# Window and linear attention with butterfly FFN on one core: the order of each instruction's waits, and where the layer norm's small steps run

## The chip, the cores and the metric

One NeuronCore of a Trainium2 chip. The metric is the device time of one launch in microseconds. The engines are PE (TensorE), DVE (VectorE), ACT (ScalarE), POOL (GpSimd) and SP, which here issues DMAs.

## The reference, cut to what matters

The input is x, 32 sequences of 256 tokens with 128 features, in float32. Four blocks with residuals run over it, each behind a layer norm without scale or shift:

```python
def _layernorm(x, axis=-1, eps=1e-05):
    m = jnp.mean(x, axis=axis, keepdims=True)
    v = jnp.var(x, axis=axis, keepdims=True)
    return (x - m) / jnp.sqrt(v + eps)

x = x + window_attention(_layernorm(x))   # 16 heads of 8, 2 KV heads, windows of 32, softmax
x = x + butterfly_ffn(_layernorm(x))      # 128 -> 512, butterfly, gelu, butterfly, -> 128
x = x + linear_attention(_layernorm(x))   # phi = elu + 1, k'v per sequence, normaliser + 1e-6
x = x + butterfly_ffn(_layernorm(x))      # the same weights again
```

The butterflies are linear and hang on the weights alone, so the kernel first multiplies them into two weight matrices (the products named `X.`), while the first tokens are already under way.

## The kernel before, in words

The 8192 tokens are cut into 16 groups of 512, each as 4 tiles of 128 tokens. A group passes through stages, and each engine works on several groups at once, shifted against each other: in its turn t an engine does, for every step, the group `t - lag`. `due(t, lag, first, last)` gives that group, and the body of each engine's `turn(t)` is the order of its steps, written out by hand. Letters name the places of a group: P (input, window attention), W (behind window attention, first FFN), F (behind the FFN, linear attention), L (behind linear attention, second FFN), G (result). `x_W` is the residual stream there, `xn_W` its normed form, `xb_W` the stream with the next bias.

Every wait between instructions is written by hand. `Count` turns "event E of group g" into a semaphore value, from tables (`PRODUCTS`, `VECTOR`, ...) that repeat the order in which an engine finishes its events. `eng.wait_ge(semaphore, value)` holds the next instruction. A machine instruction carries one wait. In the built program the one that is written first in the code rides on the instruction, and each further one becomes a wait instruction of its own ahead of it. In the listings below the last name in a `[waits ...]` list is the one that the instruction carries. Where two waits on one semaphore follow each other they are still two.

The layer norm of a group, before: DVE takes `bn_stats` of 4 tiles and `bn_aggr` of 4 tiles (`moments`, L1212 and L1217), which gives mean and variance in `mv`. POOL (`normalise`, L443 to L455) adds epsilon (`rv`), negates the mean (`nm`), raises to -0.5 (`rstd`), multiplies (`nmr`), and writes the 4 tiles of `xn`. For the first group's P and the last group's F and L, DVE writes `xn` instead (L1225). PE then transposes `xn` (L572). There are 64 such norms. DVE adds the residual (`residual`, L1240) when a product is done, ACT copies transposes out (L960) and takes gelu (L982). The softmax of a tile on DVE is: merge the halves (L1255), maximum (L1262), subtract (L1268), transpose (L1275). The heads' outputs are transposed (L1282), the sums inverted (L1286) and divided (L1289). PE writes the scores of a tile at L601 and needs for the next tile that L1268 is done.

Of the kernel before, what the change touches and what calls it, by code (L numbers as in the profile page):

```python
# [9 lines left out]
ALU = mybir.AluOpType  # L10
# [5 lines left out]
HEADS, KV, HD = 16, 2, 8  # L16
# [51 lines left out]
    ("P.bn", 1, 2, 15), ("P.mv", 1, 2, 15), ("W.max3", 3, 1, 1), ("W.cp0", 2, 0, 0), ("W.max0", 2, 0, 0), ("W.cp3", 3, 2, 15),  # L68
    ("W.cp3", 3, 0, 0), ("W.ot2", 4, 0, 1), ("W.rs2", 4, 0, 1), ("W.ot2", 4, 2, 15), ("W.rs2", 4, 2, 15), ("W.tr0", 2, 0, 0),
    ("P.bn", 0, 0, 1), ("P.mv", 0, 0, 1), ("W.max3", 3, 0, 0), ("W.max3", 3, 2, 15), ("F.bn", 5), ("F.mv", 5),  # L70
# [3 lines left out]
    ("W.tr1", 2, 0, 1), ("W.max0", 2, 2, 15), ("W.bn", 4, 0, 1), ("W.mv", 4, 0, 1), ("W.bn", 4, 2, 15), ("W.mv", 4, 2, 15),  # L74
# [18 lines left out]
NORMED = [
    ("W.xn", 5, 2, 15), ("L.xn", 7, 0, 14), ("P.xn", 0, 0, 1), ("P.xn", 1, 2, 15), ("F.xn", 5, 0, 14), ("W.xn", 4, 0, 1),
]
BIASED = [
    ("F.xb", 6), ("P.xb", 3, 2, 15), ("W.xb", 5, 0, 1), ("L.xb", 7), ("W.xb", 5, 2, 15), ("P.xb", 1, 0, 1),
]
PARTED = [
    ("W.um3", 4, 0, 0), ("W.um2", 4, 0, 1), ("W.um2", 4, 2, 15), ("W.um3", 4, 1, 15), ("W.um0", 3, 2, 15), ("W.um1", 3, 0, 1),  # L100
    ("W.um0", 2, 0, 0), ("W.um0", 3, 1, 1), ("W.um1", 3, 2, 15),
]
TURNS = NG + 14
# [8 lines left out]
    ("L.kv", "L.k0"), ("L.kv", "bank"), ("L.oT", "L.out0"), ("L.out0", "L.q"), ("L.out1", "L.kv"),  # L112
    ("L.out1", "L.q"), ("L.proj", "bank"), ("L.q", "L.xT"), ("P.kv", "bank"), ("W.PV0", "bank"),
# [21 lines left out]
class Count:  # L135
# [1474 lines left out]
```

## Time and profile before

| | |
|---|---|
| time, median of 3 runs | 561.26 us (560.38 to 562.34) |
| span of the profiled execution | 560.6 us |
| time of that execution | its span; the median of the three runs is 0.7 us above it |
| PE busy | 525.0 us |
| POOL busy | 450.9 us |
| DVE busy | 441.2 us |
| ACT busy | 358.7 us |
| mean granted TensorE clock | 0.978 of 2.4 GHz |

The span runs from the first instruction to the last. Busy time is what the engine's instructions cover. The busy end of a matmul is modelled, so that a PE without idle time is one that always had its next matmul there.

### The profile page before, as it was taken

The numbers are of one execution on the slowest core, as the hardware profiler recorded it, in microseconds if no ns is written. First come the engines' busy times: TensorE is split into PE (matmuls) and PEld (weight loads), VectorE is DVE, ScalarE is ACT, GpSimd is POOL, SyncE is SP. The second block draws the span as 40 slices with busy tenths as digits, with TensorE's granted clock in tenths as the row PEclk, the third lists the DMA queues.
The fourth block names the chain that finished last, engine by engine and source line by source line (L and its number), as shares of the span: only waits on it lengthen the run. The fifth ranks groups of instructions, "written<-read, shape, count | busy, mean of one in ns | idle before, by whom it ended". The sixth has DMA issues, their size and how long they took to land. (4 is left out here: it accounts for less than half of the span.)

```text
span 560.6 us, 14708 instructions
## 1 busy us (share of the span) xinstructions
PE 525.0 (94%) x5060; PEld 345.8 (62%) x5060; DVE 441.2 (79%) x1272; ACT 358.7 (64%) x578; POOL 450.9 (80%) x646
## 2 busy tenths in 40 slices
PE   5786998979999999999999999999999999999795
PEld 3442554546766666666667676666666667777563
DVE  5778789897888989898988898888989797663341
ACT  2543376567687767676777768686767777664532
POOL 6665689899898999999898989899999797955420
PEclk9789799989999999999999999999999999999899
DMA  9533232322223232232313231323232222100001
GB/s 310 170 76 81 63 83 54 81 74 56 54 58 80 62 76 66 68 78 48 102 45 87 63 87 44 84 60 77 61 76 50 59 66 58 39 1 20 1 20 37
DMA packets 49546, 38.88 MB, mean 69 GB/s; under 512 B 12352, under 2 KB 38976, under 8 KB 49472
## 3 DMA queue, kind: packets, MB, share of 16 engines
q1 hardware_dynamic: 47024, 33.73, 23.9%
q10 hardware_dynamic: 2448, 4.22, 2.1%
q8 instruction: 40, 0.66, 0.5%
q14 instruction: 34, 0.28, 0.2%
HBM read 15.64 MB, written 5.51 MB: 38 GB/s over the span
## 5 line engine op out<-in xcount | busy, mean ns | idle before, releaser
L501 POOL TENSOR_TENSOR probs_t<-probs_t,first 128x1024 f32<-128x1024 f32 x64 | 151.3, 2367 | 11.5 <-DMA probs_t<-probs_t 11.5
L645 PEld LDWEIGHTS ring<-w,early 128*128 128x128 f32 x1024 | 119.0, 192 | 9.6 <-issue 7.0
L982 ACT ACTIVATE early<-ring,b 128x512 f32<-128x512 f32 x128 | 87.2, 684 | 54.7 <-PE ring L633 53.1
L645 PE MATMUL ring<-w,early 128*128 128x128 f32 x1024 | 120.0, 275 | 0.8 <-ACT early L982 0.8
L972 ACT ACT_TABLE_LOAD x58 | 74.4, 1283 | 10.7 <-issue 9.7
L601 PE MATMUL ps_s<-kx,q_t 64*32 64x512 f32 x960 | 65.9, 606 | 3.4 <-DVE merged L1268 2.7
L633 PE MATMUL ring<-xT_G,w1b 128*128 128x512 f32 x128 | 67.1, 612 | 0.7 <-ACT xT_G L960 0.7
L991 ACT ACTIVATE probs_t<-merged_t 128x1024 f32<-128x1024 f32 x64 | 65.3, 1044 | 3.8 <-DVE merged_t L1275 3.7
L633 PE MATMUL ring<-xT_F,w1b 128*128 128x512 f32 x128 | 59.9, 611 | 0.4 <-ACT xT_F L960 0.4
L1255 DVE COPY_PREDICATED ps_s<-first,ps_s 128x512 f32<-128x512 uint32 x64 | 43.6, 681 | 9.2 <-PE ps_s L601 9.0
L1282 DVE STREAM_TRANSPOSE ps_o<-ps_o 128x512 f32<-128x512 f32 x64 | 46.2, 722 | 1.6 <-PE ps_o L618 0.3
L1268 DVE TENSOR_TENSOR merged<-ps_s,rowmax 128x512 f32<-128x512 f32 x64 | 44.1, 689 | 4.1
L618 PE MATMUL ps_o<-probs_t,vx 64*32 64x256 f32 x1024 | 42.3, 387 | 2.5 <-DVE o_w L1289 2.5
L1275 DVE STREAM_TRANSPOSE merged_t<-merged 128x512 f32<-128x512 f32 x64 | 44.2, 696 | 0.4
L1262 DVE TENSOR_REDUCE rowmax<-ps_s 128x16 f32<-128x512 f32 x64 | 43.2, 676 | 1.0 <-issue 0.2
L633 PEld LDWEIGHTS ring<-xT_F,w1b 128*128 128x128 f32 x128 | 23.4, 192 | 25.2 <-issue 20.4
L676 PEld LDWEIGHTS ring<-later,xT_L 128*128 128x128 f32 x128 | 23.0, 189 | 21.6 <-issue 19.0
L676 PE MATMUL ring<-later,xT_L 128*128 128x256 f32 x128 | 34.5, 392 | 0.7 <-ACT xT_L L960 0.7
L618 PEld LDWEIGHTS ps_o<-probs_t,vx 64*32 64x32 f32 x1024 | 15.3, 106 | 27.8 <-issue 22.7
L960 ACT ACTIVATE xT_F<-ring 128x512 f32<-128x512 f32 x16 | 9.6, 597 | 34.5 <-PE ring L572 34.5
L455 POOL TENSOR_SCALAR xn_W<-x_W,rstd_W,nmr_W 128x128 f32<-128x128 f32 x64 | 27.9, 451 | 3.2 <-PE ring L676 2.3
L471 POOL TENSOR_TENSOR xb_F<-x_F,later 128x512 f32<-128x512 f32 x16 | 20.6, 1285 | 12.3 <-DVE x_L L1240 12.1
(124 smaller groups left out, 1023.9 us busy)
## 6 DMA issues: line engine op xcount, KB each, us to landing
probs_t<-probs_t SPq DMA_DIRECT2D x256, 64.0 KB, 2.0
kx<-kv_rows SPq DMA_DIRECT2D x120, 40.0 KB, 2.2
x_P<-in_x SPq DMA_DIRECT2D x16, 256.0 KB, 3.2
out_x<-x_G SPq DMA_DIRECT2D x16, 256.0 KB, 2.4
vx_t<-kv_rows SPq DMA_DIRECT2D x128, 8.0 KB
up_s<-in_up_m ACTq DMA_DIRECT2D x7, 256.0 KB, 8.4
down_s<-in_down_m ACTq DMA_DIRECT2D x7, 256.0 KB, 8.4
kv_rows<-kv_t SPq DMA_DIRECT2D x16, 80.0 KB, 2.8
```

The source lines that it names most:

```text
L501: nc.gpsimd.tensor_tensor(parts, parts, keep.rearrange("p (a t) -> p a t", a=1).to_broadcast([P, PAIR * HEADS, WIN]), ALU.mult).then_inc(p ...
L601: last = nc.tensor.matmul(ps_s[32 * i:32 * i + 32, a], q_t[half, P * j + 32 * c:P * j + 32 * c + 32], keys[half, :, TSPAN * j + 32 * c:TSP ...
L618: last = nc.tensor.matmul(ps_o[32 * c:32 * c + 32, a, 0:HPK * WIN], vx[rows, j, a, s], probs_t[rows, j, s, a], start=True, stop=True)
L633: nc.tensor.matmul(bank(name)[:], w1b[:, P * c:P * (c + 1)], x_t[s][:], start=True, stop=True).then_inc(product.sem, 1)
L645: last = nc.tensor.matmul(bank(name)[:, P * j:P * (j + 1)], hid[s][:, c, P * j:P * (j + 1)], w2[:, c], start=(c == 0), stop=(c == CH - 1))
L676: last = nc.tensor.matmul(bank(name)[:, 2 * P * i:2 * P * (i + 1)], x_t["L"][:, P * j:P * (j + 1)], wl_s[:, P:3 * P], start=True, stop=True)
L972: nc.scalar.activation(unused[:, i:i + 1], half[0:1, 0:1], function)
L982: nc.scalar.activation(hid[s][:, c], bank(name)[:], ACT.Gelu, bias=b1[:, c:c + 1]).then_inc(drained[BANK[name]].sem, 1)
L991: nc.scalar.activation(probs_t[:, j].rearrange("p s k h t -> p s (k h t)"), scores.to_broadcast([P, PAIR, HEADS * WIN]), ACT.Exp).then_inc ...
L1268: nc.vector.tensor_tensor(merged[:, j % 2].rearrange("p k h t -> p (k h) t"), halves()[0], m, ALU.subtract).then_inc(drained["S"].sem, 1)
L1275: nc.vector.transpose(merged_t[:, j % 2].rearrange("p k h t -> p (k h t)"), merged[:, j % 2].rearrange("p k h t -> p (k h t)")).then_inc(v ...
L1282: nc.vector.transpose(ps_o[:, :, 0:HPK * WIN], ps_o[:, :, 0:HPK * WIN]).then_inc(vec.sem, 1)
```

## The change

Four things, and nothing else:

1. At most instructions with several waits, the order of the `wait_ge` calls is turned, so that another semaphore, as a rule that of the step just before it or of the other engine's product, is written first and rides on the instruction. Two waits on the same semaphore are joined to one with the larger value (`Count.both`).
2. Epsilon is added on DVE, right behind `bn_aggr` (`variances_raised`).
3. POOL's norm is one `rstd` and four tiles of `xn` as (x - mean) * rstd. `nm` and `nmr` are gone.
4. The turns are counted from another start (all the lags and tables change with it), and steps are written in smaller functions. In the built programs the order of instructions is the same on PE, ACT and SP, and on DVE and POOL the same but for points 2 and 3.

The core of the diff:

```diff
+    def both(self, *events):
+        return max(self.value(group, name) for group, name in events)
...
+            def rooted_variance(g, s):
+                pool.wait_ge(vec.sem, vec.after(g, f"{s}.rv"))
+                if g == 0:
+                    pool.wait_ge(half_set, 1)
+                nc.gpsimd.tensor_tensor(rstd[s][:], rv[s][:], half[:], ALU.pow).then_inc(rooted.sem, 1)
             def normalise(g, s):
-                pool.wait_ge(vec.sem, vec.after(g, f"{s}.mv"))
-                pool.wait_ge(pool_step.sem, pool_step.after(g - 1, f"{s}.nmr"))
-                nc.gpsimd.tensor_scalar(rv[s][:], mv[s][:, :, 1], LN_EPS, None, ALU.add
-                                        ).then_inc(pool_step.sem, 1)
-                nc.gpsimd.tensor_scalar(nm[s][:], mv[s][:, :, 0], -1.0, None, ALU.mult).then_inc(pool_step.sem, 1)
-                pool.wait_ge(pool_step.sem, pool_step.after(g, f"{s}.rv"))
-                nc.gpsimd.tensor_tensor(rstd[s][:], rv[s][:], half[:], ALU.pow).then_inc(pool_step.sem, 1)
-                pool.wait_ge(pool_step.sem, pool_step.after(g, f"{s}.nm", f"{s}.rstd"))
-                nc.gpsimd.tensor_tensor(nmr[s][:], nm[s][:], rstd[s][:], ALU.mult).then_inc(pool_step.sem, 1)
...
+                rooted_variance(g, s)
+                pool.wait_ge(rooted.sem, rooted.after(g, f"{s}.rstd"))
                 pool.wait_ge(product.sem, product.after(g - 1, TURNED[s]))
-                pool.wait_ge(pool_step.sem, pool_step.after(g, f"{s}.nmr"))
                 for j in range(TILES):
-                    last = nc.gpsimd.tensor_scalar(xn[s][:, j], x_of(g, s)[:, j], rstd[s][:, j:j + 1],
-                                                   nmr[s][:, j:j + 1], ALU.mult, ALU.add)
+                    last = nc.gpsimd.tensor_scalar(xn[s][:, j], x_of(g, s)[:, j], mv[s][:, j, 0:1],
+                                                   rstd[s][:, j:j + 1], ALU.subtract, ALU.mult)
...
             def copy_out(g, name, dst, *freed):
-                act.wait_ge(product.sem, product.after(g - 1, *freed))
-                act.wait_ge(product.sem, product.after(g, name))
+                act.wait_ge(product.sem, product.both((g, name), *((g - 1, user) for user in freed)))
...
             def gelu(g, s, c):
+                act.wait_ge(product.sem, product.both((g, name), (g - 1, f"{s}.down")))
                 if g == 0:
                     act.wait_ge(b1_made, 1)
-                act.wait_ge(product.sem, product.after(g - 1, f"{s}.down"))
-                act.wait_ge(product.sem, product.after(g, name))
...
+            def variances_raised(g, s):
+                dve.wait_ge(vec.sem, vec.after(g, f"{s}.mv"))
+                nc.vector.tensor_scalar(rv[s][:], mv[s][:, :, 1], LN_EPS, None, ALU.add).then_inc(vec.sem, 1)
...
             def residual(g, s, name, base):
+                dve.wait_ge(product.sem, product.after(g, name))
                 if s == "G":
+                    dve.wait_ge(biased.sem, biased.after(g, f"{base}.xb"))
                     dve.wait_ge(y_out.sem, y_out.after(g - 1, "G.y"))
                 else:
+                    dve.wait_ge(biased.sem, biased.both((g, f"{base}.xb"), (g - 1, f"{s}.xb")))
                     dve.wait_ge(normed.sem, normed.after(g - 1, f"{s}.xn"))
-                    dve.wait_ge(biased.sem, biased.after(g - 1, f"{s}.xb"))
-                dve.wait_ge(biased.sem, biased.after(g, f"{base}.xb"))
-                dve.wait_ge(product.sem, product.after(g, name))
...
             def row_max(g, j):
+                dve.wait_ge(vec.sem, vec.after(g, f"W.cp{j}"))
                 dve.wait_ge(drained["S"].sem, drained["S"].after(g - 1, f"W.S{j}"))
-                dve.wait_ge(vec.sem, vec.after(g, f"W.cp{j}"))
```

The wait instructions that stand by themselves go from 355 to 79 on ACT, from 638 to 527 on DVE, from 200 to 140 on POOL, from 65 to 63 on SP and from 248 to 251 on PE.

VectorE in a middle turn, before, from the residual at F to the norm of L; each row is an instruction with its line, its tile and what it waits for:

```order
L1240 TENSOR_TENSOR x_F<-ring,xb_W 128x512 [waits biased,product,normed]
L1212 BN_STATS stats_F<-x_F 128x6 [waits vector_result,drained_3]
L1217 BN_AGGR mv_F<-stats_F 128x2 [waits vector_result,normed]
L1311 TENSOR_SCALAR norm<-ring 128x32 [waits product]
L1314 RECIPROCAL rnorm<-norm 128x32 [waits vector_result]
L1317 TENSOR_TENSOR o_l<-ring,rnorm 128x256 [waits vector_result,product]
L1282 STREAM_TRANSPOSE ps_o<-ps_o 128x2x256 [waits product]
L1286 RECIPROCAL recip<-ps_o 128x16 [waits vector_result,drained_T]
L1289 TENSOR_TENSOR o_w<-ps_o,recip 128x128 [waits vector_result,product]
```

The same place of the changed kernel:

```order
L1172 TENSOR_TENSOR x_F<-ring,xb_W 128x512 [waits normed,biased,product]
L1138 BN_STATS stats_F<-x_F 128x6 [waits vector_result,drained_3]
L1145 BN_AGGR mv_F<-stats_F 128x2 [waits normed,vector_result]
L1151 TENSOR_SCALAR rv_F<-mv_F 128x4 [waits vector_result]
L1245 TENSOR_SCALAR norm<-ring 128x32 [waits product]
L1250 RECIPROCAL rnorm<-norm 128x32 [waits vector_result]
L1255 TENSOR_TENSOR o_l<-ring,rnorm 128x256 [waits product,vector_result]
L1212 STREAM_TRANSPOSE ps_o<-ps_o 128x2x256 [waits product]
L1217 RECIPROCAL recip<-ps_o 128x16 [waits drained_T,vector_result]
L1222 TENSOR_TENSOR o_w<-ps_o,recip 128x128 [waits product,vector_result]
```

No row has moved; `rv_F` has come in, and the wait that stands last in a list, which the instruction carries, is now the one on the step just before it (`vector_result`) or on PE's product.

GpSimd, the norm of the last group at L, before:

```order
L443 TENSOR_SCALAR rv_L<-mv_L 128x4
L445 TENSOR_SCALAR nm_L<-mv_L 128x4
L447 TENSOR_TENSOR rstd_L<-rv_L,half 128x4
L449 TENSOR_TENSOR nmr_L<-nm_L,rstd_L 128x4
L455 TENSOR_SCALAR xn_L<-x_L,rstd_L,nmr_L 128x128 x4
```

The same norm of the changed kernel:

```order
L444 TENSOR_TENSOR rstd_L<-rv_L,half 128x4
L452 TENSOR_SCALAR xn_L<-x_L,mv_L,rstd_L 128x128 x4
```

Three of the eight instructions are gone from GpSimd's queue, one of them to VectorE; the neighbours on both sides are the same.

## Rows read from the trace of the kernel before

**Rows 1.** The page: busy time of PE, and the granted clock in 40 slices.

```profile
PE 525.0 (94%) x5060; PEld 345.8 (62%) x5060; DVE 441.2 (79%) x1272; ACT 358.7 (64%) x578; POOL 450.9 (80%) x646
PEclk9789799989999999999999999999999999999899
```

**Rows 2.** Stretches: their us, busy PE, PEld, DVE, ACT, POOL, clock, DMA.

```profile
0.00:148.50 148.50, 124.19 (x1184) 71.64 (x1185) 119.80 (x328) 77.47 (x126) 114.53 (x158) 0.93 0.37 101
178.74:208.97 30.23, 30.23 (x309) 20.28 (x308) 26.54 (x79) 21.98 (x35) 27.82 (x41) 1.00 0.29 73
148.50:420.60 272.10, 272.10 (x2773) 182.50 (x2772) 238.98 (x694) 198.89 (x315) 250.32 (x361) 1.00 0.28 70
420.60:515.00 94.40, 94.04 (x885) 66.61 (x885) 67.61 (x201) 65.18 (x108) 75.47 (x110) 1.00 0.17 43
515.00:560.60 45.60, 34.66 (x223) 25.03 (x221) 14.83 (x52) 17.11 (x29) 10.55 (x19) 0.96 0.07 18
```

**Rows 3.** Groups by line: count, busy us, mean ns, then idle us before them.

```profile
L1286 DVE RECIPROCAL recip<-ps_o 128x16 f32<-128x16 f32 x64 | 16.5, 258 | 6.9 <-DVE ps_o L1282 0.5
L1314 DVE RECIPROCAL rnorm<-norm 128x32 f32<-128x32 f32 x32 | 11.3, 353 | 1.1
L1311 DVE TENSOR_SCALAR norm<-ring 128x32 f32<-128x32 f32 x32 | 5.2, 164 | 7.2 <-PE ring L726 7.1
L998 ACT ACTIVATE phi_k<-neg_k 128x256 f32<-128x256 f32 x32 | 13.3, 417 | 1.0
L455 POOL TENSOR_SCALAR xn_L<-x_L,rstd_L,nmr_L 128x128 f32<-128x128 f32 x60 | 26.2, 450 | 2.7 <-POOL nmr_L L449 2.4 <-PE ps_s L601 0.2 <-PE ps_o L618 0.2
```

**Rows 4.** The chain that ended last: start us, us, what.

```profile
547.94 0.02 issue
...
548.03 0.61 ACT xT_G L960
...
557.07 0.03 issue
...
557.19 0.69 DVE x_G L1240
```

**Rows 5.** Timeline of the last norm: start us, us, instruction [idle before].

```profile
543.98 0.38 DVE L1217 BATCH_NORM_AGGREGATE mv_L<-stats_L 128x2 f32<-128x6 f32 x4
544.45 0.24 POOL L443 TENSOR_SCALAR rv_L<-mv_L 128x4 f32<-128x4 f32 x1 [7.26 <-DVE mv_L L1217]
544.97 1.04 POOL L447 TENSOR_TENSOR rstd_L<-rv_L,half 128x4 f32<-128x4 f32 x1
546.09 0.20 POOL L449 TENSOR_TENSOR nmr_L<-nm_L,rstd_L 128x4 f32<-128x4 f32 x1
546.10 1.12 DVE L1225 TENSOR_SCALAR xn_L<-x_L,mv_L,rstd_L 128x128 f32<-128x128 f32 x4 [1.74 <-issue]
```

**Rows 6.** Timeline before the middle: what PE waits longest for.

```profile
116.93 0.38 DVE L1217 BATCH_NORM_AGGREGATE mv_W<-stats_W 128x2 f32<-128x6 f32 x4
118.14 0.24 POOL L443 TENSOR_SCALAR rv_W<-mv_W 128x4 f32<-128x4 f32 x1
121.96 0.66 PE L572 MATMUL ring<-first,xn_W 128*128 128x128 f32 x4 [2.69 <-POOL xn_W L455]
```

**Rows 7.** Waits of PE from 0 to 150 us: total us, times, longest.

```profile
PE ring L572 <- POOL xn_W L455: 3.9, 2, 2.7
PE ps_s L601 <- DVE merged L1268: 3.3, 6, 1.0
PE ps_o L618 <- DVE o_w L1289: 2.5, 2, 2.1
```

**Rows 8.** Waits of PE's weight loads from 150 to 420 us.

```profile
PEld ps_s L601 <- DVE merged L1268: 1.5, 9, 0.2
```

**Rows 9.** Timeline: GpSimd beside a VectorE tensor-scalar, second norm.

```profile
12.91 0.84 DVE L312 TENSOR_SCALAR d_tmp<-d_t,outer 128x128 f32<-128x128 f32 x4
13.08 0.51 POOL L443 TENSOR_SCALAR rv_P<-mv_P 128x4 f32<-128x4 f32 x1 [4.50 <-DVE mv_P L1217]
```

More of the change, by code:

```diff
@@ L464, in add_bias @@
                         pool.wait_ge(bffn_made, 1)
-                behind = 2 if s == "P" else 1
-                pool.wait_ge(drained[BANK[used]].sem, drained[BANK[used]].after(g - behind, used))
                 if source is None:
@@ new lines, in turn @@
+                for g in due(t, 5):
+                    add_bias(g, "F", bproj_s, "F.down", "L.proj")
+                for g in due(t, 2, 2):
+                    add_bias(g, "P", bo_s, None, "W.proj")
+                for g in due(t, 4, 2):
+                    normalise(g, "W")
+                for g in due(t, 3, 0, 1):
+                    probs_parted(g, 2)
+                for g in due(t, 4, 0, 1):
+                    add_bias(g, "W", bffn_s, "W.proj", "F.down")
+                for g in due(t, 6, 0, 14):
+                    normalise(g, "L")
@@ new lines, in turn @@
+                for g in due(t, 3, 2):
+                    probs_parted(g, 2)
+                for g in due(t, 6):
+                    add_bias(g, "L", bffn_s, "L.proj", "G.down")
+                if t == 20:
+                    rooted_variance(15, "L")
+                for g in due(t, 4, 2):
+                    add_bias(g, "W", bffn_s, "W.proj", "F.down")
+                if t == 19:
+                    rooted_variance(15, "F")
+                for g in due(t, 3, 1):
+                    probs_parted(g, 3)
@@ L779, in turn @@
-                for g in due(t, 7, 2, 15):
+                for g in due(t, 3, 2):
                     scores(g, 1)
+                if t == 5:
+                    weighted_values(1, 0)
+                    up_transposed()
+                    weighted_values(1, 1)
+                for g in due(t, 6):
+                    linear_kv_rows(g, 0)
+                    linear_q(g)
+                    linear_kv_rows(g, 1)
+                for g in due(t, 8, 0, 14):
+                    ffn_down(g, "G")
@@ new lines, in turn @@
+                for g in due(t, 5):
+                    norm_transposed(g, "F", "W")
+                for g in due(t, 3, 2):
+                    scores(g, 2)
+                for g in due(t, 4, 2):
+                    weighted_values(g, 1)
+                for g in due(t, 6):
+                    linear_state(g)
+                for g in due(t, 5):
+                    ffn_up(g, "F", 3)
+                    ffn_up(g, "F", 2)
+                    ffn_up(g, "F", 0)
+                    ffn_up(g, "F", 1)
@@ new lines, in turn @@
+                for g in due(t, 6, 0, 14):
+                    linear_out(g, 0)
+                for g in due(t, 7):
+                    norm_transposed(g, "G", "L")
+                if t == 21:
+                    linear_out(15, 0)
+                for g in due(t, 3, 1):
+                    scores(g, 3)
+                for g in due(t, 4):
+                    weighted_values(g, 2)
+                for g in due(t, 2, 2):
+                    attention_q(g)
+                for g in due(t, 5):
+                    ffn_down(g, "F")
@@ L791, in turn @@
-                for g in due(t, 10):
-                    linear_kv_rows(g, 0)
-                if t == 8:
+                    up_stage(3, "a")
+                    up_stage(3, "b")
+                    up_stage(4, "a")
+                    scores(0, 2)
+                    up_stage(5, "a")
+                    down_stage(1)
+                    scores(0, 3)
+                    attention_q(1)
+                    weighted_values(0, 0)
+                    down_stage(2)
+                    up_stage(4, "b")
@@ new lines, in turn @@
+                    scores(1, 0)
+                    up_stage(6, "a")
+                if t == 0:
+                    up_stage(2, "a")
+                    first_keys(1)
+                    scores(0, 0)
+                    norm_transposed(1, "P", "P")
+                    down_stage(0)
+                for g in due(t, 4, 0, 1):
+                    weighted_values(g, 3)
+                for g in due(t, 6, 0, 14):
+                    linear_out(g, 1)
+                for g in due(t, 7, 0, 14):
+                    ffn_up(g, "G", 3)
@@ new lines, in turn @@
+                if t == 21:
+                    linear_out(15, 1)
+                for g in due(t, 1, 2):
+                    norm_transposed(g, "P", "P")
+                if t == 4:
+                    heads_transposed(0)
+                if t == 3:
+                    down_stage(3)
+                    scores(1, 1)
+                    down_stage(4)
+                for g in due(t, 4, 2):
+                    weighted_values(g, 3)
+                for g in due(t, 2, 2):
+                    scores(g, 0)
@@ L934, in turn @@
-                if t == 27:
-                    ffn_up(15, "G", 3)
+                    up_stage(5, "b")
+                for g in due(t, 7):
+                    ffn_up(g, "G", 0)
+                if t == 22:
+                    ffn_up(15, "G", 3)
+                    ffn_up(15, "G", 2)
+                    ffn_down(15, "G")
+                for g in due(t, 6):
+                    linear_transposed(g)
+                for g in due(t, 7, 0, 14):
+                    ffn_up(g, "G", 2)
+                for g in due(t, 4, 1):
+                    heads_transposed(g)
@@ L1028, in attention_q_out @@
             def attention_q_out(g):
+                act.wait_ge(product.sem, product.both((g, "P.q"), *((g - 1, user) for user in SCORES)))
                 if g == 0:
                     act.wait_ge(first_in, 16)
-                act.wait_ge(product.sem, product.after(g - 1, *SCORES))
-                act.wait_ge(product.sem, product.after(g, "P.q"))
                 nc.scalar.activation(q_t[:], bank("P.q")[:], ACT.Identity, bias=bq_s[:]
@@ L1125, in turn @@
+                for g in due(t, 4, 0, 14):
                     gelu(g, "G", 3)
-                for g in due(t, 11):
+                for g in due(t, 4):
                     gelu(g, "G", 0)
-                for g in due(t, 10):
+                if t == 19:
+                    gelu(15, "G", 3)
+                    gelu(15, "G", 2)
+                for g in due(t, 3):
                     copy_out(g, "L.oT", o_lt[:], "L.proj")
-                if t == 6:
-                    down_stage_out(2)
@@ L1187, in attention_kv_out @@
             def attention_kv_out(g):
+                dve.wait_ge(product.sem, product.after(g, "P.kv"))
                 if g == 0:
@@ L1209, in moments @@
                     dve.wait_ge(x_in[g % 2], 16 * (g // 2 + 1))
+                else:
+                    own = drained[BANK[MADE[s]]]
+                    dve.wait_ge(own.sem, own.after(g, MADE[s]))
                 dve.wait_ge(vec.sem, vec.after(g - 1, f"{s}.mv"))
@@ L1241, in residual @@
                                         xb_of(g, base)[:].rearrange("p j n -> p (j n)"), ALU.add).then_inc(own.sem, 1)
-                if s != "G":
-                    dve.wait_ge(own.sem, own.after(g, name))
             def halves():
@@ L1487, in turn @@
                     subtract_max(g, 2)
-                for g in due(t, 2, 2, 15):
+                if t == 3:
+                    heads_turned(0, 1)
+                    sums_inverted(0, 1)
+                    heads_divided(0, 1)
+                    merge_halves(1, 3)
+                if t == 2:
+                    values_out(0)
+                for g in due(t, 2, 2):
                     scores_transposed(g, 1)
```

708 lines of the change are left out of this document (266 added, 442 removed), and 76 rows, old and new, of tables (COVERED, PRODUCTS, VECTOR).

## Prediction

> **What bounds the kernel now.** I read the page first, then the stretches, then PE's waits, and last the timeline where PE does wait. The page has PE busy for 525.0 of 560.6 us [rows 1]. An average says little, so the stretches come next [rows 2]. From 148.5 to 420.6 us PE is busy in all of the 272.10 us, at full clock. A turn there takes 30.235 us (one of the nine alike is shown), and VectorE and GpSimd fill only 26.5 and 27.8 us of it. In that stretch no matmul waits for anybody; only weight loads do, by 0.2 us at most [rows 8], under cover of the matmul before. So the middle belongs to PE's own work, and no faster hand-over changes it. PE is idle elsewhere: 148.50 - 124.19 = 24.3 us while the pipeline fills, 0.4 us from 420.6 to 515, and 45.60 - 34.66 = 10.9 us while it drains. These 36 us are all that the change can reach. In the fill the waits are for the norm of W on GpSimd, the softmax and the heads' outputs on VectorE [rows 7]. In the drain one norm after another stands on the chain that ends last [rows 4, 5].
>
> **A wait that rides on its instruction.** RECIPROCAL stands in two groups. At L1286 the step that it needs is the wait instruction ahead of it, and the idle time is 6.9 / 64 = 108 ns; at L1314 it needs only the step before it, which it carries, and it is 1.1 / 32 = 34 ns [rows 3]. The change makes the first kind into the second: 0.074 us for each VectorE step that waits for the one before (`mv`, maximum, subtract, `recip`, `o_w`, `o_l`). On ACT a copy starts 548.03 - 547.94 = 0.09 us after PE's product with two waits [rows 4], and a step with one wait 1.0 / 32 = 0.03 us after ACT's own [rows 3]; I take 0.06 us. A residual starts 557.19 - 557.07 = 0.12 us after the product [rows 4]; I take 0.08 us from it. Bounds: zero, if the second wait isn't what costs, and the whole gap. The two like groups speak for the full difference. On PE three separate waits are added, and there I count nothing: PE's sequencer is ahead of the array, and where the cover is gone (PE idle) I found no row that tells the two kinds apart.
>
> **The norm.** From the end of `mv_L` (543.98 + 0.38 = 544.36) to `rstd_L` (544.97) go 0.61 us for two small GpSimd steps [rows 5]. Afterwards it is a hop on VectorE of 0.034, the small addition there, and 0.09 to GpSimd (544.36 to 544.45). The trace has no such addition; its nearest row is the TENSOR_SCALAR of 128x32, 0.164 us [rows 3], and 128x4 can't take longer, while 0.1 is as low as I would go. That makes 0.29, so 0.32 us less. Behind `rstd` (ends 546.01) GpSimd needs `nmr` to 546.29 and a gap of 2.4 / 13 = 0.18 us before `xn` [rows 3, 5], 0.46 in all; afterwards one gap of 0.08 (as before `nmr`) to 0.18. I take 0.18, so 0.28 us less. A norm of GpSimd's queue alone goes from 544.45 to 546.29 + 0.18 = 2.02 us ahead of `xn` down to 1.04 + 0.18 = 1.22, so 0.80 us less. The four `xn` tiles change their two operations; with no row for the new pair I leave them at 0.450 us [rows 3], bounds 0.40 and 0.50.
>
> The added step costs VectorE 0.034 + 0.164 = 0.2 us, four times a turn, 0.8 us. Against it stand some 17 shorter hops a turn, 1.2 us. VectorE comes out even or a little earlier, and has 3.7 us of a turn free.
>
> **The port.** GpSimd's small step beside a VectorE TENSOR_SCALAR took 0.51 us [rows 9], and beside none 0.24 [rows 5]. The added TENSOR_SCALAR is such an instruction, but covers 0.16 us; at 0.27 us each with five norms on the path the sum below would be 1.3 us smaller, and that is in the range. The Trainium skill speaks against the change here: "Advanced Engine Details and Errata", VectorE Performance Modes, says that VectorE's second SBUF port is shared with GPSIMD, and that 2-port instructions and GPSIMD's block each other. By that rule all 64 additions can hold up GpSimd; the trace shows it for one longer one.
>
> **The sum.** Drain: two norms (F and L of the last group, DVE writes `xn`) 2 x 0.32; their `mv`, twice `o_l`, once `kvs`, 5 x 0.074; three residuals x 0.08; two copies and a gelu x 0.06. That is 0.64 + 0.37 + 0.24 + 0.18 = 1.4 us. Fill up to 57 us: the path runs through softmax and heads' steps on VectorE, some 16 hops x 0.074 = 1.2, less one added step 0.2, plus the norm that PE waits for there, 0.6: 1.6 us, and 0.3 for the ACT and VectorE hops before it. Fill from 57 us: one norm at W near 94 us, 0.32 + 0.28 and five hops, 1.0 us. Then GpSimd's norms of P, F and W come without a pause between its other work. They end in PE's longest wait, 2.69 us [rows 6]: GpSimd gains 3 x 0.80 = 2.4. But `mv_W` ends at 117.31 and `rv_W` starts at 118.14 [rows 6], so that only 0.83 us of the delay before it is GpSimd's own; with what VectorE gains (0.3) and the norm itself (0.32 + 0.28) it is 0.83 + 0.3 + 0.6 = 1.7. With 0.2 near 64 us the fill gives 1.9 + 0.2 + 1.0 + 1.7 = 4.8 us. Middle: 0. Span 560.6 - 1.4 - 4.8 = 554.4; the median of the runs lies 0.7 above the span, so **555.1 us**, I say 555.0.
>
> **The rivals.**
> - *The wait's place is nothing.* Then only the norms gain: 0.64 in the drain, 0.6 + 0.6 + 0.8 + 0.6 in the fill, 3.2 us: 558.0. Against it: 108 and 34 ns on the same operation. 12%.
> - *The clock.* The fill has a mean clock of 0.93 [rows 2], so 0.14 of 148.5 us, 21 us, at 1.2 GHz, which costs 10.4 us; the slices below 9 stand where PE idles [rows 1]. Less idling may give back a third: 551.5, 8%. Work that moves into such a stretch may lose 3 us: 558, 5%. The Trainium skill, "TensorE: Matmul & The Clock Gate", Part 1, has the throttled state as the default that activity releases; by it the first is the likelier.
> - *The middle isn't PE's.* If the repeated 30.23 us were a loop through VectorE or GpSimd, each of 13 turns would give about 1 us: 542. Against it: no wait of a matmul in 272 us. 4%.
> - *Slower.* The softmax step `merged` releases PE's next weight load with 0.17 us of waiting in each middle turn [rows 8]; the matmul behind has little more cover than 0.1 us. If VectorE came later there by more than that (the 0.8 us of additions with no gain from the waits, less the cover), PE would stall 0.6 us a turn, 13 x 0.6 = 8 us: 569. Against it: VectorE waits for PE just before, at the residual of L, and takes up the delay. 5%.
> - *Nothing arrives*, because the freed time meets DMAs or the port: 560. 4%.
>
> The forecast itself has 62%, with a range of its own of 552 to 558.
>
> **How the numbers follow.** About 0.3% (1.7 us) is what a measurement of this kernel can tell from no change; faster therefore means below 559.6. The range 551.0 to 559.0 leaves out the middle's 4%, the slower and the empty case, and some of the tails. Faster: the forecast, the clock and the middle whole, and most of the first rival, 0.86. Same: the empty case and rests of the others, 0.08. Slower: 0.06.
>
> **What the changed profile would show.** PE 30.23 us of 30.23 a turn as before. Gaps of 34 instead of 108 ns before `recip`, `o_w`, `o_l`. `mv` to `rstd` 0.29 instead of 0.61 us. PE's wait for `xn_W` at about 117 to 119 us, with 1.0 us or more gone from 2.69. PE idle in the drain about 9.5 instead of 10.9. The prediction is wrong if the middle turn's length changes, if `xn` on GpSimd leaves 0.45 us, or if the fill keeps its 24 us of idle time.

## The result, and the profile after

The changed kernel takes 570.12 us (median of 4 runs, 568.40 to 571.20) against 561.25 us before. The ratio is 1.0152, with a 95% interval of 1.0121 to 1.0183: slower by 8.9 us, where 555.0 had been forecast with a range of 551.0 to 559.0. The execution profiled after has a span of 567.5 us at a mean clock of 0.988, against 560.6 us at 0.978. Where a kernel ran often, an execution more than 1.5% above its fastest is left out of the ratios: one of twelve of `e13_waits_again` (562.6 us) and one of the 23 of the kernel before beside the last runs (564.3 us).

The page after: busy time, the granted clock in 40 slices, and the shares of the chain that ended last.

```profile
PE 525.2 (93%) x5060; PEld 344.1 (61%) x5060; DVE 485.8 (86%) x1336; ACT 358.4 (63%) x578; POOL 492.7 (87%) x454
PEclk9898998989999999999999999999999999999999
POOL 60%; PE 17%; issue 14%; SPq 3%; DVE 3%; ACTq 1%; ACT 1%; DMA 0%; POOLq 0%; DVEq 0%
```

PE's busy time is that of [rows 1]. GpSimd has 192 instructions fewer and is busy 41.8 us more; VectorE has 64 more and is busy 44.6 us more. The chain runs over GpSimd for 60% of the span.

The stretches after, in the columns of [rows 2]:

```profile
0.00:148.50 148.50, 122.59 (x1190) 70.88 (x1191) 126.86 (x349) 78.72 (x130) 124.34 (x116) 0.95 0.36 102
198.50:229.89 31.39, 30.71 (x309) 20.40 (x310) 30.57 (x82) 22.07 (x35) 30.65 (x29) 1.00 0.26 65
148.50:420.60 272.10, 266.44 (x2692) 177.31 (x2690) 264.95 (x700) 191.77 (x304) 265.79 (x244) 1.00 0.27 67
```

The second is one turn, with as many matmuls (309) as the turn of [rows 2] and 31.39 us long instead of 30.23. PE now idles in the middle, by 5.7 us of 272.1. GpSimd's busy time in a turn went from 27.82 to 30.65 us and VectorE's from 26.54 to 30.57. Eleven turns have this length (31.39 to 31.43 us). What PE waits for there, from 150 to 420 us, in the columns of [rows 7]:

```profile
PE ring L630 <- DVE x_F L1172: 4.4, 9, 0.5
PE ring L572 <- POOL xn_F L452: 1.3, 8, 0.2
```

Each comes once a turn: first VectorE's residual, then GpSimd's norm. The waits themselves don't say which engine sets the pace.

Counted from GpSimd's third `probs_t` of a group, the changed kernel is 4.3 us ahead at the start of the eleven and 10.4 us behind at their end, and has won 3.5 us of that back by the end of the span.

The groups of GpSimd and VectorE that grew, after, in the columns of [rows 3]:

```profile
L452 POOL TENSOR_SCALAR xn_W<-x_W,mv_W,rstd_W 128x128 f32<-128x128 f32 x64 | 49.9, 793 | 1.7
L1151 DVE TENSOR_SCALAR rv_P<-mv_P 128x4 f32<-128x4 f32 x16 | 19.1, 1194 | 0.5
L1151 DVE TENSOR_SCALAR rv_F<-mv_F 128x4 f32<-128x4 f32 x16 | 17.5, 1094 | 0.6
L1151 DVE TENSOR_SCALAR rv_W<-mv_W 128x4 f32<-128x4 f32 x16 | 11.7, 732 | 0.6
L1151 DVE TENSOR_SCALAR rv_L<-mv_L 128x4 f32<-128x4 f32 x16 | 2.9, 180 | 0.5
L1217 DVE RECIPROCAL recip<-ps_o 128x16 f32<-128x16 f32 x64 | 16.5, 257 | 2.2
```

An `xn` tile takes 793 ns, and took 450. The added `rv` takes 1194, 1094, 732 and 180 ns by place, where its own work is 169 ns. In front of `recip` the idle time fell from 6.9 to 2.2 us, that is from 108 to 34 ns each, as the prediction had it.

The timeline after, in a middle turn:

```profile
198.82 2.37 POOL L498 TENSOR_TENSOR probs_t<-probs_t,first 128x1024 f32<-128x1024 f32 x1
199.64 1.58 DVE L1151 TENSOR_SCALAR rv_F<-mv_F 128x4 f32<-128x4 f32 x1
201.14 0.18 DVE L1245 TENSOR_SCALAR norm<-ring 128x32 f32<-128x32 f32 x1
201.30 1.03 POOL L444 TENSOR_TENSOR rstd_F<-rv_F,half 128x4 f32<-128x4 f32 x1
202.43 3.12 POOL L452 TENSOR_SCALAR xn_F<-x_F,mv_F,rstd_F 128x128 f32<-128x128 f32 x4
...
230.22 2.37 POOL L498 TENSOR_TENSOR probs_t<-probs_t,first 128x1024 f32<-128x1024 f32 x1
```

`rv_F` starts 0.82 us after GpSimd's `probs_t` and ends some 25 ns after it does (199.64 + 1.58 = 201.22; 198.82 + 2.37 = 201.19). So do all 36 of the 64 that take over 0.3 us: they end 23 to 32 ns after the GpSimd instruction beside them, a TENSOR_TENSOR in 35 cases and a MEMSET in one. Fourteen `rv_L` lie inside GpSimd's TENSOR_SCALAR of `xn_W` instead, and take 175 to 186 ns. GpSimd has no pause in the turn but the hops (the gaps between the end of the step that is waited for and the start of the next, seven of 0.10 to 0.11 us, 0.74 us in all), and the same step comes again after 230.22 - 198.82 = 31.40 us: its queue is full.

The last norm and PE's longest wait for `xn`, after, which answer to [rows 5] and [rows 6, 7]:

```profile
551.50 0.38 DVE L1145 BATCH_NORM_AGGREGATE mv_L<-stats_L 128x2 f32<-128x6 f32 x4
551.91 0.17 DVE L1151 TENSOR_SCALAR rv_L<-mv_L 128x4 f32<-128x4 f32 x1
552.16 1.03 POOL L444 TENSOR_TENSOR rstd_L<-rv_L,half 128x4 f32<-128x4 f32 x1 [7.10 <-DVE rv_L L1151]
```

```profile
PE ring L572 <- POOL xn_W L452: 5.4, 3, 3.2
```

From the end of `mv_L` to `rstd_L` go 552.16 - 551.88 = 0.28 us, where 0.29 was forecast and 0.61 stood. PE's longest wait for `xn_W` is 3.2 us, though; it was 2.7, and the four tiles ahead of it take 1.4 us longer.

### The profile page after: what moved, and what is told of

Same layout as the page of the kernel before. It is cut to its first block, busy times and chain, and to the rows that moved or that the text cites. A ratio compares the mean times of both kernels' runs of the same rounds, so it can differ in the third digit from the quotient of the medians.

```text
span 567.5 us, 14134 instructions
## 1 busy us (share of the span) xinstructions
PE 525.2 (93%) x5060; PEld 344.1 (61%) x5060; DVE 485.8 (86%) x1336; ACT 358.4 (63%) x578; POOL 492.7 (87%) x454
## 4 chain that ended last, share of the span: by engine, by line
POOL 60%; PE 17%; issue 14%; SPq 3%; DVE 3%; ACTq 1%; ACT 1%; DMA 0%; POOLq 0%; DVEq 0%
POOL probs_t L498 15%; POOL xn_F L452 7%; POOL xn_W L452 7%; POOL xn_P L452 7%; POOL xn_L L452 6%; PE ring L630 5%; PE ring L642 4%; POOL rstd_W L444 3%; POOL xb_W L468 3%; POOL rstd_F L444 3%; POOL xb_L L468 2%; POOL xb_P L468 2%; POOL rstd_P L444 2%; POOL rstd_L L444 2%; SPq L382 2%
## 5 line engine op out<-in xcount | busy, mean ns | idle before, releaser
L940 ACT ACTIVATE early<-ring,b 128x512 f32<-128x512 f32 x128 | 86.0, 681 | 53.3 <-PE ring L630 52.2
L452 POOL TENSOR_SCALAR xn_W<-x_W,mv_W,rstd_W 128x128 f32<-128x128 f32 x64 | 49.9, 793 | 1.7
L452 POOL TENSOR_SCALAR xn_P<-x_P,mv_P,rstd_P 128x128 f32<-128x128 f32 x60 | 47.3, 801 | 1.6
L452 POOL TENSOR_SCALAR xn_L<-x_L,mv_L,rstd_L 128x128 f32<-128x128 f32 x60 | 46.8, 794 | 1.6
L452 POOL TENSOR_SCALAR xn_F<-x_F,mv_F,rstd_F 128x128 f32<-128x128 f32 x60 | 46.8, 794 | 1.6
```

The costliest lines, as they stand in the source:

```text
L452: last = nc.gpsimd.tensor_scalar(xn[s][:, j], x_of(g, s)[:, j], mv[s][:, j, 0:1], rstd[s][:, j:j + 1], ALU.subtract, ALU.mult)
L940: nc.scalar.activation(hid[s][:, c], bank(name)[:], ACT.Gelu, bias=b1[:, c:c + 1]).then_inc(drained[BANK[name]].sem, 1)
```

## The experiments

Three theories stood after this. **A:** the `xn` tiles of 794 ns have made GpSimd's queue longer than PE's work. **B:** `rv` on VectorE, held until GpSimd's instruction ends, is what lengthens the turn. **C:** the new order of waits costs.

### One part undone at a time

`e1_xn_back` brings `nm` and `nmr` back on GpSimd and keeps `rv` on VectorE:

```diff
+                nc.gpsimd.tensor_scalar(nm[s][:], mv[s][:, :, 0], -1.0, None, ALU.mult).then_inc(rooted.sem, 1)
...
                 nc.gpsimd.tensor_tensor(rstd[s][:], rv[s][:], half[:], ALU.pow).then_inc(rooted.sem, 1)
...
+                nc.gpsimd.tensor_tensor(nmr[s][:], nm[s][:], rstd[s][:], ALU.mult).then_inc(rooted.sem, 1)
...
-                    last = nc.gpsimd.tensor_scalar(xn[s][:, j], x_of(g, s)[:, j], mv[s][:, j, 0:1],
-                                                   rstd[s][:, j:j + 1], ALU.subtract, ALU.mult)
+                    last = nc.gpsimd.tensor_scalar(xn[s][:, j], x_of(g, s)[:, j], rstd[s][:, j:j + 1],
+                                                   nmr[s][:, j:j + 1], ALU.mult, ALU.add)
```

> After, with GpSimd's norm made as before (nm, rstd, nmr and xn as a product and a sum), the wait order and the addition rv on VectorE kept. Three theories. A, the xn tiles (794 ns against 451) made GpSimd the bound of the middle (a turn of 31.39 us in which it has no idle time): xn falls back to 0.45 us, GpSimd gives 4 x (4 x 0.34 - 0.43 - 0.2) = 3.0 us a turn back, the turn returns to PE's 30.24 us, and the time is 556 to 558 us. B, VectorE's rv, which ends only when the GpSimd instruction beside it ends (1.58 us for rv_F, 1.85 for rv_P), is the bound by itself: the turn stays above 30.7 us and the time is 563 or more. C, the order of waits costs: 568 or more.

Measured: 553.76 us, ratio to before 0.9869 (0.9835 to 0.9903). The middle of this kernel, and its `xn`:

```profile
148.50:420.60 272.10, 272.10 (x2780) 182.82 (x2772) 245.37 (x730) 198.69 (x316) 241.54 (x325) 1.00 0.28 69
L463 POOL TENSOR_SCALAR xn_W<-x_W,rstd_W,nmr_W 128x128 f32<-128x128 f32 x64 | 27.8, 449 | 1.7
```

PE is busy in all of the 272.10 us again, and `rv` takes 170 to 253 ns. Making `xn` as before takes away the whole loss and brings the time 7.6 us under that of before, lower than the 556 to 558 that A expected. C falls. A and B both still stand, since `rv` has stopped waiting in the same run.

`e2_rv_back` does the opposite: `rv` back on GpSimd, ahead of `rstd`, with the new `xn`.

```diff
+                nc.gpsimd.tensor_scalar(rv[s][:], mv[s][:, :, 1], LN_EPS, None, ALU.add).then_inc(rooted.sem, 1)
...
                 nc.gpsimd.tensor_tensor(rstd[s][:], rv[s][:], half[:], ALU.pow).then_inc(rooted.sem, 1)
```

> After, with rv back on GpSimd ahead of rstd, the new xn form and the wait order kept. A (GpSimd is the bound through xn): every norm puts about 0.24 + 0.1 us more on a queue that is already full, so a turn is 31.39 + 4 x 0.34 = 32.8 us and the time 585 to 589 us, the slowest of all. B (rv on VectorE is the bound): VectorE is freed of 4.6 us a turn and the time falls below 561 us. C (order of waits): about 570.

Measured: 578.86 us, ratio 1.0322 (1.0274 to 1.0371). One turn:

```profile
199.70:232.01 32.31, 30.73 (x308) 20.31 (x308) 26.51 (x78) 22.08 (x35) 31.56 (x33) 1.00 0.26 63
```

VectorE has 4 us of a turn less to do, and the turn grows by 0.92 us to 32.31, which is GpSimd's added work (31.56 - 30.65 = 0.91). The expected 32.8 and 585 were too high: they counted 0.1 us a norm for a further hop, but GpSimd's gaps in a turn are 0.75 us in all here and were 0.74, so the hop behind `rv` only takes the place of the one from VectorE. VectorE's load is not what sets the turn.

`e3_waits_only` undoes both edits of the norm and keeps the wait order; `e13_waits_again` is the same kernel once more.

> The wait order alone: both edits of the norm undone (rv, nm, rstd, nmr on GpSimd, xn as a product and a sum). If the order of waits gives what the shorter hops say (34 instead of 108 ns on VectorE), the fill and the drain give some 3 us and the time is 557 to 558.5. If a wait's place is worth nothing: 561. If the new order is what costs (theory C): 565 to 570. A and B both allow the first.

> e3_waits_only once more, beside e10_dve_order's kernel on one chip, since half a per cent is in question: 555 if its time holds, and e10_dve_act_order above it by what VectorE's and ACT's order are worth together: 2 to 4 us by theory, 0 if a wait's place is nothing.

Measured: 555.06 us, 0.9885 (0.9856 to 0.9913), and 553.55 us, 0.9893 (0.9860 to 0.9927). The wait order alone goes with a gain of 6 us, twice the expected; how much of it is the order itself is taken up in the part on the prediction.

### Which property of xn costs

`e4_forms` adds a tail behind the last store that times forms of the instruction (its total of 628.4 us means nothing). The code of the first two of its ten forms:

```diff
+            for r in range(3):
+                nc.gpsimd.tensor_scalar(o[:, r], x0, one, two, ALU.mult, ALU.add)
+            for r in range(3, 6):
+                nc.gpsimd.tensor_scalar(o[:, r], x0, mean, two, ALU.subtract, ALU.mult)
```

> After, with a tail behind the last store that no part of the result needs: ten forms of a GpSimd TENSOR_SCALAR of 128x128 f32, three times each, and then nine forms of a small VectorE instruction, twice each, each started 0.1 us behind the start of a GpSimd product of 128x1024 f32 that takes some 2.4 us. The question is which property costs. For GpSimd: if it is the subtraction ahead of the product, the forms with the mean packed (stride 1) and with an addition ahead of the product tell whether it is the subtraction (add, mult 0.45; subtract, mult 0.79) or the sum ahead of the product (both 0.79); if it is the operand with stride 2, mult, add with such an operand takes 0.79 too. For VectorE: a TENSOR_SCALAR of 128x4 between SBUF tensors takes some 2.2 us (to the end of GpSimd's product); if only the strided input does that, the packed one takes 0.17. A TENSOR_TENSOR of the same size and a reduction over statistics should take under 0.3 us, as o_w and mv do beside GpSimd's work in the kernel.

GpSimd's groups in the tail. L572 is multiply then add, L574 subtract then multiply with the mean at stride 2, L576 the same with it packed, L578 add then multiply, L582 multiply then subtract; L586 is a single subtraction, L588 a single product:

```profile
L582 POOL TENSOR_SCALAR early<-kx,m_one,m_two 128x128 f32<-128x128 f32 x3 | 2.4, 795 | 0.0
L574 POOL TENSOR_SCALAR early<-kx,m_mv,m_two 128x128 f32<-128x128 f32 x3 | 2.3, 794 | 0.0
L576 POOL TENSOR_SCALAR early<-kx,m_one,m_two 128x128 f32<-128x128 f32 x3 | 2.3, 792 | 0.0
...
L586 POOL TENSOR_SCALAR early<-kx,m_one 128x128 f32<-128x128 f32 x3 | 1.8, 603 | 0.0
L588 POOL TENSOR_SCALAR early<-kx,m_one 128x128 f32<-128x128 f32 x3 | 1.8, 604 | 0.0
L572 POOL TENSOR_SCALAR early<-kx,m_one,m_two 128x128 f32<-128x128 f32 x3 | 1.3, 448 | 0.1
L578 POOL TENSOR_SCALAR early<-kx,m_one,m_two 128x128 f32<-128x128 f32 x3 | 1.3, 448 | 0.0
```

It is the subtraction as one of two operations, in either place: 792 to 795 ns, against 448 for pairs of sums and products. The stride of the operand and the order of the two don't matter. Subtract then multiply with two constants in place of the operands from tiles (L590) took 645 ns, so the kind of operand counts as well; why was not tested. The VectorE half of this run failed: the small instructions began 45 ns ahead of GpSimd's product and mostly met nothing.

`e7_add_nm` puts that into the changed kernel. Only `nm` comes back, and the sum stays ahead of the product:

```diff
-                    last = nc.gpsimd.tensor_scalar(xn[s][:, j], x_of(g, s)[:, j], mv[s][:, j, 0:1],
-                                                   rstd[s][:, j:j + 1], ALU.subtract, ALU.mult)
+                    last = nc.gpsimd.tensor_scalar(xn[s][:, j], x_of(g, s)[:, j], nm[s][:, j:j + 1],
+                                                   rstd[s][:, j:j + 1], ALU.add, ALU.mult)
```

> After, with xn as (x + nm) * rstd, where nm = -mean is made on GpSimd ahead of rstd (0.23 us); rv stays on VectorE, nothing else changes. If a subtraction among the two operations is what makes a tile take 794 ns, a tile now takes 448 ns with its sum still ahead of its product and two operands still read from tiles; a turn is PE's 30.24 us and the time 552 to 555, about that of e1_xn_back (553.8) or 0.5 us less, since nmr is gone. If another property of the new form costs (the sum first), the time stays near 570.

Measured: 554.35 us, 0.9883 (0.9840 to 0.9926), `xn` tiles of 447 to 454 ns, a turn of 30.24 us. The only differences from the changed kernel are the operation and one small GpSimd step more, and they are worth 15 us by the ratios, 16 by the medians. Here, too, `rv` waits no more (170 to 213 ns), so what its waiting adds is a question for the next runs.

### What holds rv, and what that costs

`e5_port` repeats the failed half with a BATCH_NORM_STATS2 ahead of each form, so that the form begins 165 ns after the start of GpSimd's instruction.

> After, with a tail behind the last store that no part of the result needs. In e4_forms the small VectorE instructions began 45 ns ahead of GpSimd's product, so that most of them told nothing. Here each stands behind a BATCH_NORM_STATS2 of 0.29 us and so begins some 0.25 us behind the start of GpSimd's 1.9 us product. Theory: the addition rv (TENSOR_SCALAR, 128x4, source and result in SBUF) then ends with GpSimd's product, after some 1.6 us, every time, and so do its packed form, a copy and a SCALAR_TENSOR_TENSOR of two SBUF tiles; one with three columns, one with its source in PSUM, the statistics and the reduction take 0.2 to 0.3 us. Open is TENSOR_TENSOR of 128x4 with two SBUF inputs: if it takes 0.16 us, it is a form of rv that doesn't wait. The last six stand beside a GpSimd TENSOR_SCALAR (like xn) in place of the product. Rival: only the strided input waits, then the packed one takes 0.17 us.

VectorE's groups beside GpSimd's TENSOR_TENSOR of 1.89 us (L1507 with three columns, L1509 TENSOR_TENSOR of two SBUF tiles, L1505 `rv`'s form packed, of which one of the two lies ahead of the view's window, L1515 its source in PSUM), and in the second list beside a GpSimd TENSOR_SCALAR of 1.20 us:

```profile
L1507 DVE TENSOR_SCALAR kx<-m_one 128x3 f32<-128x3 f32 x2 | 3.5, 1751 | 0.0
L1519 DVE COPY kx<-m_one 128x4 f32<-128x4 f32 x2 | 3.5, 1750 | 0.0
...
L1509 DVE TENSOR_TENSOR kx<-m_mv,m_two 128x4 f32<-128x4 f32 x2 | 3.5, 1744 | 0.0
L1505 DVE TENSOR_SCALAR kx<-m_one 128x4 f32<-128x4 f32 x1 | 1.8, 1751 | 0.0
L1523 DVE BATCH_NORM_STATS2 kx<-kx 128x6 f32<-128x128 f32 x2 | 0.6, 276 | 0.0
L1517 DVE RECIPROCAL kx<-m_one 128x4 f32<-128x4 f32 x2 | 0.3, 160 | 0.0
L1521 DVE TENSOR_REDUCE kx<-kx 128x4 f32<-128x16 f32 x2 | 0.3, 153 | 0.0
L1515 DVE TENSOR_SCALAR kx<-ps_s 128x4 f32<-128x4 f32 x2 | 0.3, 144 | 0.0
```

```profile
L1505 DVE TENSOR_SCALAR kx<-m_one 128x4 f32<-128x4 f32 x2 | 0.3, 152 | 0.0
L1509 DVE TENSOR_TENSOR kx<-m_mv,m_two 128x4 f32<-128x4 f32 x2 | 0.3, 146 | 0.0
```

TENSOR_SCALAR and copy from SBUF to SBUF, and TENSOR_TENSOR of two SBUF tiles, wait for the end of GpSimd's TENSOR_TENSOR, however small they are (three columns too, against the expectation; `rv`'s own form with its source at stride 2, L1503, took 1751 ns as well). A source in PSUM, RECIPROCAL, the reduction and the statistics don't wait. Beside GpSimd's TENSOR_SCALAR none of the three forms tried waits, as `rv_L` beside `xn_W` showed in the kernel. The Trainium skill, "SBUF — State Buffer", Who interferes with whom, has VectorE and GpSimd take a shared port pair for a whole instruction, in order of issue, and lists the same kinds on VectorE's side; the trace agrees there. By the same section a GpSimd TENSOR_SCALAR would hold them up as well, and these rows don't show that.

`e6_rv_tt` was laid out before this was known: `rv` in the changed kernel as a TENSOR_TENSOR with a tile of epsilon.

> After, with VectorE's rv as a TENSOR_TENSOR with a tile that holds epsilon, instead of a TENSOR_SCALAR; all else kept, the xn tiles of 794 ns too. If GpSimd's own work sets the turn (theory A), the turn stays at 31.4 us and the time at 568 to 571, whether this form of rv waits for GpSimd or not. If rv doesn't wait any more and VectorE was the bound (B), VectorE has 4 us of a turn less to do and the time is 562 or less.

Measured: 568.93 us, 1.0142 (1.0098 to 1.0187), turn 31.38 us. `rv` waits as before (`rv_F` 1103 ns), so the run tells nothing on A or B.

`e11_rv_reduce` uses the form that doesn't wait. Epsilon stands in a third column of `mv`; `xn` stays as changed.

```diff
-                nc.vector.tensor_scalar(rv[s][:], mv[s][:, :, 1], LN_EPS, None, ALU.add).then_inc(vec.sem, 1)
...
+                nc.vector.tensor_reduce(rv[s][:], mv[s][:, :, 1:3], AX_X, ALU.add).then_inc(vec.sem, 1)
```

> After, with rv made by a TENSOR_REDUCE (a sum over variance and an epsilon that stands beside it in mv), a form that did not wait for GpSimd's product in e5_port (153 ns). The xn tiles keep their 794 ns. Theory A (GpSimd's queue alone sets the turn of 31.4 us): VectorE's busy time of a turn falls by 4 us, the turn stays, and the time is 568 to 571. If rv's waiting held up the turn (B), the time falls below 566.

Measured: 564.90 us, 1.0105 (1.0066 to 1.0144). A turn, and GpSimd in it at the place of the timeline above:

```profile
195.93:226.96 31.03, 30.66 (x309) 20.28 (x308) 27.27 (x82) 22.10 (x35) 30.61 (x29) 1.00 0.27 65
```

```profile
195.93 2.38 POOL L501 TENSOR_TENSOR probs_t<-probs_t,first 128x1024 f32<-128x1024 f32 x1
198.27 1.03 POOL L447 TENSOR_TENSOR rstd_F<-rv_F,half 128x4 f32<-128x4 f32 x1
```

A's 568 to 571 was missed, and by B's mark (below 566) `rv`'s waiting does hold up the turn. VectorE is 3.3 us of a turn lighter, GpSimd's busy time is unchanged, and yet the turn is 0.36 us shorter. In the changed kernel `rv_F` can only end behind `probs_t`, and GpSimd stands still from 201.19 to 201.30 for the hand-over; here `rstd_F` follows without a gap. Three norms of a turn have this gap of 0.11 us: 0.33 us. So B is true for that third of the excess (31.39 - 30.23 = 1.16 us a turn), and A for the rest; and B only on top of A, since in `e7_add_nm` and the next run, where GpSimd has slack, it costs nothing.

`e12_nm_reduce` joins `e7_add_nm` and this form of `rv`.

> e7_add_nm (xn as a sum and a product with nm from GpSimd) with rv by the same TENSOR_REDUCE. In e7_add_nm the rv of P and L took 0.21 and 0.20 us in place of 0.17, so at most 2 us of waiting in all is left to save, most of it hidden: 553 to 554.5, within what can be told from e7_add_nm (554.4). Under 551 would say that rv's waiting mattered in the fill.

Measured: 553.91 us, 0.9896 (0.9852 to 0.9940): no difference from `e7_add_nm`. With GpSimd's queue short enough, the waiting costs nothing that can be told here; little was left of it in `e7_add_nm` to save.

### Where the wait order pays

`e9_dve_order` is `e3_waits_only` with VectorE's pairs of waits turned back; `e10_dve_act_order` turns back ACT's as well.

```diff
+                dve.wait_ge(drained["T"].sem, drained["T"].after(g if j >= 2 else g - 1, f"W.PV{(j - 2) % 4}"))
                 dve.wait_ge(vec.sem, vec.after(g, f"W.ot{j}"))
-                dve.wait_ge(drained["T"].sem, drained["T"].after(g if j >= 2 else g - 1, f"W.PV{(j - 2) % 4}"))
...
-                act.wait_ge(product.sem, product.both((g, name), *((g - 1, user) for user in freed)))
+                act.wait_ge(product.sem, product.after(g - 1, *freed))
+                act.wait_ge(product.sem, product.after(g, name))
```

> e3_waits_only with the order of two waits turned back on VectorE alone, in front of mv, maximum, subtract, the transposes of the scores, recip, o_w and o_l: the step before on VectorE is waited for last again. Theory: each of these begins 108 ns instead of 34 ns behind the one before; 16 such steps on the path of the fill and 5 in the drain give 21 x 0.074 = 1.6 us, and the time is 556.5 to 557.5 against 555.1 of e3_waits_only. If the gain of 6.3 us of e3_waits_only comes from these steps in full: 560 to 562. If a wait's place doesn't matter there: 555.

> e9_dve_order with ACT's waits turned back as well: the product of the turn before and PE's new product are waited for apart, the new one last, so that an ACT instruction begins some 97 ns behind PE's product instead of 37. Theory: the gain of the wait order over the kernel before (6.3 us in e3_waits_only, some of it clock) sits largely here, since e9_dve_order kept it; ACT stands between PE's matmuls on the path of the fill some 30 times: 557 to 559. If ACT's order is worth nothing either: 555, and the rest of the gain is with PE, GpSimd and the residuals, or with the clock.

Measured: 555.21 us, 0.9909 (0.9874 to 0.9944), and 556.66 us, 0.9950 (0.9921 to 0.9980), the latter beside `e13_waits_again` with 0.9893. In the first, the idle time before `recip` is back at 103 ns:

```profile
L1226 DVE RECIPROCAL recip<-ps_o 128x16 f32<-128x16 f32 x64 | 16.5, 258 | 6.6
```

Both engines' orders together are worth 0.57%, about 3.2 us, within the 2 to 4 expected, with intervals that all but part; at equal clocks (0.985, 0.988 and 0.994) `e10_dve_act_order` is 1.9, 3.1 and 2.7 us slower than `e13_waits_again`. VectorE's alone (0.24%, some 1.3 us, against 1.6 expected) can't be told from zero: its 555.21 us is what was expected if the place didn't matter there. Nor can its share be told from ACT's.

## Why the prediction was wrong

**The step that failed** is the last sentence on GpSimd's norm: "The four `xn` tiles change their two operations; with no row for the new pair I leave them at 0.450 us, bounds 0.40 and 0.50." They take 0.794 us. In a turn that is 16 x 0.344 = 5.5 us more, against 4 x (0.24 + 0.23 + 0.20) = 2.7 us that leave GpSimd, which makes 27.8 + 2.8 = 30.6 us of busy time, the 30.65 that the trace shows. With the 0.74 us of hops that the changed kernel's turn shows this is 31.39. The same sum gives the point where GpSimd overtakes PE's 30.24: (30.24 - 0.74 - 27.8 + 2.7) / 16 = 0.275 us more per tile, so at 0.725. The bounds had ended well below it, with nothing behind them but the row of another pair. Without the hops, which no row of before gives for the new norm, the same sum has the point at 0.77, so that the rows that were there would have found it nearly as well; the prediction never set GpSimd's turn after the change against PE's.

**The middle** ("Middle: 0") fell with it. It was right that PE bounded it before, and `e1_xn_back` has PE busy in 272.10 of 272.10 us again; but a bound belongs to the load of all engines, and the change moved GpSimd's. That `xn` leaving 0.45 us would make the forecast wrong had been said, without a price. All three signs of being wrong came: the turn changed, `xn` left 0.45, and the fill kept its idle time (148.50 - 122.59 = 25.9 us).

**The added step** ("0.2 us, four times a turn, 0.8 us") cost VectorE 51.2 us in place of 12.8 in all. The port was weighed the wrong way round: only as VectorE's addition holding up a GpSimd step by 0.27 us. Here the one that comes second waits, and where the two met, in 36 of 64 norms, the addition was second. Its price was 0.36 us a turn, 4.0 us over eleven turns. The times agree roughly: `e11_rv_reduce` is 5.2 us faster than the changed kernel by the medians (570.1 to 564.9) and 2.6 us by the ratios to before, whose intervals overlap. It was paid because GpSimd was full: between `e7_add_nm` and `e12_nm_reduce` no such gain shows.

**The waits.** The hops were right: 34 ns for 108 before `recip` (means), and on ACT 37 ns for 97 between PE's product and a copy (medians over the traces of `e3_waits_only` and before). Their sum in the forecast is 3.0 us (the rival that leaves them out says 558.0 against 555.0), and `e3_waits_only` measured 6.3. A part of that goes with the clock. Over 22 runs of the kernel before that stood beside the last four experiments, the time falls from 562.7 us at a mean clock of 0.979 to 555.3 at 0.993, 4.6 us for each 0.01 by a fitted line. At equal clocks the kernel before takes 4.6 us more than `e13_waits_again` at 0.985, 5.4 at 0.988 (a single run of the latter) and 3.5 at 0.991. So 3.5 to 5 us are the wait order, somewhat above the forecast's 3.0. The rest comes with a clock that is higher in most runs; the rival that expected this ("551.5, 8%") had the right direction, though which of clock and time follows the other these runs don't show. Why less idling in the fill goes with a higher clock was not tested.

**The norm's small steps.** `mv` to `rstd` is 0.28 us as forecast. The 3.2 us that these steps were to bring are not there: `e7_add_nm` and `e12_nm_reduce`, in which GpSimd's norm is two steps shorter and `xn` is fast, take 554.4 and 553.9 us, `e3_waits_only` with the old norm 555.1 and 553.6. Up to a microsecond can hide in that. The largest term, 1.7 us at PE's longest wait for `xn_W` in the fill, can be followed in the traces. In the waits of `e13_waits_again` and then of `e12_nm_reduce`, the longest at that place is

```profile
PE ring L585 <- POOL xn_W L465: 3.6, 2, 2.5
PE ring L581 <- DVE phi_k L1241: 2.5, 1, 2.5
```

Before it is 2.69 us, with the waits alone 2.5, and with the shorter norm 2.5 again, but now VectorE's `phi_k` ends it: there `xn_W` is done at 115.50 us, `phi_k` at 116.71, and PE starts at 116.85. In the kernel before, `phi_k` ended at 121.45 us, only 0.46 ahead of `xn_W` at 121.91. So of the 1.7 us that the prediction took there, no more than about 0.5 was to be had from `xn_W` alone, as long as `phi_k` came no sooner: the wait that would end last once `xn_W` came sooner was not looked for. The 3.2 us are not all accounted for by this.

**The rivals.** The slower case had the right size, 569 us, by luck, from another mechanism: `merged`, on which it rested, no longer stands among the waits of PE or its weight loads in the middle (150 to 420 us) at all, and GpSimd's own queue was not among the rivals.

## What to carry to other kernels

When an instruction changes its operations, treat its duration as unknown, and work out from which duration on its engine would overtake the bound: if that point lies near the nearest row (here 0.725 us against 0.450), it is a case of its own, and one small timing run settles it. Before a shortened wait is counted in full, look for the wait that would end last there without it (here it ended only 0.46 us earlier). Before a small step is moved to VectorE to relieve GpSimd, look at what GpSimd runs at that moment. The changed kernel with `xn` as (x + nm) * rstd is 15 to 16 us faster than with (x - mean) * rstd, and 6 us faster than the kernel before.

## What the runs showed of the hardware

- GpSimd's TENSOR_SCALAR of 128x128 f32 with operands from tiles: 448 ns with two operations of sum and product, 792 to 795 with a subtraction among them, and 603 to 604 with a single operation, more than with two sums or products (`e4_forms`).
- VectorE's SBUF-to-SBUF TENSOR_SCALAR, copy and TENSOR_TENSOR of 128x3 or 128x4 end 17 to 26 ns after a GpSimd TENSOR_TENSOR that began before them; beside a GpSimd TENSOR_SCALAR the first and the last take their 145 to 152 ns (`e5_port`). A GpSimd MEMSET held one `rv_P` of the changed kernel too: 892 ns.
- `recip` starts 34 ns behind VectorE's step before it where it carries that wait, and 108 where the wait stands ahead of it; a copy on ACT starts 37 and 97 ns behind PE's product.
- The mean clock of a run and its time go together in this kernel: 0.01 more, 4.6 us less (22 runs of the kernel before).
